# Six attention layers on one core: the transposed probabilities leave PSUM in two copies instead of one

## Chip, core and metric

The kernel runs on one core of one Trainium2 chip. Its metric is the device time of one launch in microseconds (us). Three runs of the kernel before gave 2954.64 us in the median, from 2952.83 to 2957.69.

## What is computed

The network has a first block (16-head attention on 2048 tokens of 128 features, beside an 8-expert layer) and a second block. The second block adds two branches: a selective-scan (Mamba) branch, and six transformer layers. The change lies in the attention of those six layers. Cut to that part, the reference is:

```python
def local_attention(q, k, v):              # WINDOW 32, 16 heads of 64
    bk2, bv2 = (look(bk), look(bv))        # each window of 32 sees itself and the one before
    sim = jnp.einsum('bhwie,bhwje->bhwij', bq, bk2) * QK_SCALE
    sim = jnp.where(mask, -jnp.finfo(sim.dtype).max, sim)
    attn = jax.nn.softmax(sim, -1)
    out = jnp.einsum('bhwij,bhwje->bhwie', attn, bv2)
...
for i in range(DEPTH):                     # DEPTH 6
    x = attn_layer(shift_tokens(x), Wqkv[i], q_scale[i], k_scale[i], Wo[i]) + x
    x = ffn_layer(shift_tokens(x), ln_g[i], ln_b[i], W1[i], b1[i], W2[i], b2[i]) + x
```

Each q and k row is also normalised per head and turned by rotary tables.

## The kernel before

The part that matters here begins some 1190 us into the run. `transformer_pe`, `transformer_dve`, `transformer_act`, `transformer_pool` and `transformer_sp` each write one engine's instruction stream for 96 steps (6 layers of 16 tiles of 128 tokens), and 7 more steps in which only the feed-forward part of the last tiles is left. The order inside a step is written out by hand and is the same in every step. The engines are tied by semaphores alone.

PSUM is used as four pairs of banks (`pair_table`). A pair is 128 partitions by two banks of 512 fp32. On TensorE the helper `pair(key, *until)` names the next user of a pair: it first waits for what the user before had left as `until`, and then stores its own `until` for the one to come.

TensorE (PE) does in step n, in this order:

- `scores_first(n)`: the mask and half of the scores of tile n
- `project_q(n + 2)`, then `scores_second(n)`
- `side(n)`: one transpose, and the output projection of tile n - 1 (line 1438)
- `project_k(n + 2)`
- `turn_probs(n)`: eight 128x128 transposes of the probabilities `k.pr` into a pair (line 1386), four into each bank. The first four wait for the first half of the exponentials and the next four for the second half (`exp`)
- `project("v", n + 1)` (line 1345, 128x512 matmuls)
- `values(n, 0)`: 32 products with 64x32 weight blocks, which the trace lists as 64 matmuls (line 1396). They read chunks 0 to 3 of `k.prT`
- `forward(n)`: a piece of the feed-forward part (lines 1444 to 1459) that cycles over four steps: in steps 0, 1 and 3 of each four two 128x512 products, in step 2 `down` and four transposes. It writes to the pair that held the turned probabilities. In the first six steps there is none
- `values(n, 1)`: the same as `values(n, 0)` on chunks 4 to 7
- `turn_rows` for q and k of tile n + 1 (line 1353), and `turn_out(n)` (line 1405)

VectorE (DVE) does in step n: a scan of the Mamba branch (line 468, from step 22), `shift(n)` (a maximum over the scores, line 1807, and two subtractions, line 1813), `finish(n - 1)` (line 1853), `rotate("q", n + 2)` (lines 1826 to 1828), `turn_probs(n)` (line 1846, the copy of the turned probabilities from PSUM to `k.prT` in SBUF), `rotate("k", n + 2)`, `normalise(n, 0)` and `normalise(n, 1)` (lines 1798 and 1802, which divide the values by the sums of the probabilities), then sums of squares for tile n + 2 (lines 1835 and 1840) and a remainder of the feed-forward part.

ScalarE (ACT) takes the exponential in two halves (`probs`, line 1650), and copies the turned rows of q and k and the turned output.

Of the kernel before, what the change touches and what calls it, by code (L numbers as in the profile page):

```python
# [92 lines left out]
def bcast(ap, at, n):  # L93
    shape = list(ap.shape)
    return ap.unsqueeze(at).broadcast_to(shape[:at] + [n] + shape[at:])
# [1230 lines left out]
def transformer_pe(k):  # L1326
    E, s, ps = k.te, k.sem, k.ps
    held = {}

    def pair(key, *until):  # L1330

        p = k.pair[key]
        for name, value in held.get(p, ()):
            E.wait_ge(s(name), value)
        held[p] = until
        return ps[:, 2 * p:2 * p + 2, :]
# [42 lines left out]
        score_half(n, 1, ps[:, 2 * p:2 * p + 2, :]).then_inc(s("lscore"), 1)  # L1379

    def turn_probs(n):
        to = pair(("turn_probs", n), ("prT", n + 1))
        for c in range(8):
            if c % 4 == 0:
                E.wait_ge(s("exp"), 2 * n + c // 4 + 1)
            mm = E.transpose(to[:, c // 4, c % 4 * P:(c % 4 + 1) * P], k.pr[:, c * P:(c + 1) * P], k.ident[:])  # L1386
        mm.then_inc(s("prob_mm"), 1)

    def values(n, o):
        to = pair((f"values{o}", n), (f"on{o}", n + 1))  # L1390
        E.wait_ge(s("prT"), n + 1)
        E.wait_ge(s(f"vw{n % 2}"), 160 * (n // 2 + 1))
        for c in range(4):
            for w in range(4):
                for i in range(2):
                    mm = E.matmul(to[WIN * w:WIN * (w + 1), i, c * (DH + 1):(c + 1) * (DH + 1)],  # L1396
                                  k.prT[i * DH:(i + 1) * DH, 4 * o + c, WIN * w:WIN * (w + 1)],
                                  k.vw[i * DH:(i + 1) * DH, n % 2, w, 4 * o + c, :], start=True, stop=True, skip_group_check=True)
        mm.then_inc(s(f"values{o}"), 1)
# [145 lines left out]
    for n in range(LAST_STEP):  # L1545
# [10 lines left out]
        if n < NTILE:  # L1556
            turn_probs(n)
        if n + 1 < NTILE:
            project("v", n + 1, ("v_out", n + 2))
        if n < NTILE:  # L1560
            values(n, 0)
# [5 lines left out]
        if n < NTILE:  # L1567
            values(n, 1)
# [216 lines left out]
def transformer_dve(k):  # L1785
    V, s, ps = k.ve, k.sem, k.ps

    def pair(*key):
        p = k.pair[key]
        return ps[:, 2 * p:2 * p + 2, :]  # L1790

    def heads(*key):
        return pair(*key).rearrange("p a (h d) -> p (a h) d", d=DH)
# [11 lines left out]
    def shift(n):  # L1805
        V.wait_ge(s("lscore"), n + 1)
        V.tensor_reduce(k.nmxl[:], heads("scores", n), X_AXIS, ALU.max, negate=True).then_inc(s("v"), k.v.up())
        V.wait_ge(s("v"), k.v.n)
        if n:
            V.wait_ge(s("prob_mm"), n)  # L1810
        for o in range(2):
            of = slice(8 * o, 8 * o + 8)
            V.tensor_tensor(k.pr[:].rearrange("p (h d) -> p h d", d=DH)[:, of, :], heads("scores", n)[:, of, :], bcast(k.nmxl[:, of], 2, DH), ALU.add).then_inc(s("shifted_s"), 1)
# [26 lines left out]
        V.tensor_reduce(k.sx[:, n % 2, :], k.ss[:, n % 2, :, :], X_AXIS, ALU.max).then_inc(s("squares"), 1)  # L1840

    def turn_probs(n):
        V.wait_ge(s("prob_mm"), n + 1)
        if n:
            V.wait_ge(s("values1"), n)
        V.tensor_copy(k.prT[:].rearrange("p c n -> p (c n)"), pair("turn_probs", n).rearrange("p a b -> p (a b)")).then_inc(s("prT"), 1)

    def finish(n):
        l, t = n // NT, n % NT
# [45 lines left out]
    for n in range(LAST_STEP):  # L1895
# [5 lines left out]
        if n < NTILE:  # L1901
            shift(n)
# [8 lines left out]
        if n < NTILE:  # L1911
            turn_probs(n)
# [364 lines left out]
```

## Time and profile before

| | us |
|---|---|
| Median of three runs | 2954.64 |
| The profiled execution, its own time | 2953.88 |
| Its span in the trace | 2951.7 |
| TensorE busy in the span | 2796.9 |
| VectorE busy in the span | 2318.7 |

The span is what the trace shows from its first to its last instruction. The time of an execution is 2.18 us more. TensorE's granted clock averaged 0.992 of full speed (2.4 GHz). Start times in the rows below are us from the start of the span.

### The profile page before, as it was taken

What the parts mean: (1) busy time and instruction counts of PE and PEld (TensorE: products, weight loads), DVE (VectorE), ACT (ScalarE), POOL (GpSimd) and SP (SyncE); (2) the same over time, 40 slices, a digit from 0 to 9 for tenths busy, and PEclk for the clock granted to TensorE, in tenths of its full rate; (3) what the DMA queues carried; (4) which work ended last, traced back from release to release, by engine and by line L of the source; (5) the groups of instructions that cost most, each with busy time, mean ns of one, the idle gap of its engine ahead of it and who ended that gap; (6) DMA issues with size and microseconds to landing.
All of it is one profiled execution on the core that took longest, in us unless ns stands there. A gap on an engine that the chain in (4) does not pass through costs nothing.

```text
span 2951.7 us, 98080 instructions
## 1 busy us (share of the span) xinstructions
PE 2796.9 (95%) x40886; PEld 1837.8 (62%) x40886; DVE 2318.7 (79%) x3704; ACT 1755.5 (59%) x2626; POOL 1677.4 (57%) x1458
## 2 busy tenths in 40 slices
PE   8999999999999998889999999999999999999995
PEld 5556566555665655566666666666666666666664
DVE  6777756684677777989868898889988998888982
ACT  4455555555666665556566666666666666666662
POOL 1000002000566665666667888788887888788872
PEclk9999999999999999999999999999999999999998
DMA  2000000000011121243243434333433343333431
GB/s 95 1 1 1 1 1 3 1 1 10 24 45 47 44 47 45 57 133 76 68 126 85 96 88 117 83 96 90 114 92 82 88 115 93 90 92 85 92 76 47
DMA packets 183064, 188.20 MB, mean 64 GB/s; under 512 B 77470, under 2 KB 130468, under 8 KB 181092
## 3 DMA queue, kind: packets, MB, share of 16 engines
q1 hardware_dynamic: 182628, 181.94, 24.7%
q8 instruction: 328, 5.37, 0.8%
q14 instruction: 108, 0.88, 0.1%
HBM read 61.00 MB, written 6.03 MB: 23 GB/s over the span
## 4 chain that ended last, share of the span: by engine, by line
PE 75%; DVE 11%; issue 5%; SPq 3%; POOL 3%; ACT 2%; DMA 1%; DVEq 0%; POOLq 0%; ACTq 0%
PE ps L1345 14%; PE ps L579 12%; PE ps L1353 5%; PE ps L1396 5%; PE ps L1438 5%; PE ps L1360 4%; PE ps L614 4%; PE ps L592 4%; PE ps L1386 3%; PE ps L1459 2%; PE ps L1405 2%; PE ps L1452 2%; PE ps L526 2%; PE ps L597 2%; DVE nmx L687 2%
## 5 line engine op out<-in xcount | busy, mean ns | idle before, releaser
L1345 PE MATMUL ps<-wqkv,xcT 128*128 128x512 f32 x1152 | 552.7, 602 | 5.8 <-issue 2.4
L579 PE MATMUL ps<-xnT,qp 128*128 128x512 f32 (+3 forms) x1280 | 526.0, 542 | 18.4 <-ACT prob L806 17.6
L1966 POOL TENSOR_TENSOR ra<-ra,rb 128x1024 f32<-128x1024 f32 x191 | 451.3, 2368 | 122.5 <-DVE rb L1828 121.6
L806 ACT ACTIVATE prob<-ps,ebias,shift 128x1024 f32<-128x1024 f32 (+7 forms) x384 | 360.3, 954 | 125.9 <-DVE ebias L696 57.1
L814 ACT ACTIVATE probT<-ps 128x512 f32<-128x512 f32 (+3 forms) x384 | 207.7, 541 | 351.3 <-PE ps L592 351.2
L579 PEld LDWEIGHTS ps<-xnT,qp 128*128 128x128 f32 x1280 | 231.5, 190 | 274.1 <-issue 229.5
L1985 POOL TENSOR_TENSOR ra<-ra,rn 128x1024 f32<-128x1024 f32 x192 | 362.3, 1908 | 8.9 <-DVE ra L1893 1.2
L687 DVE TENSOR_REDUCE nmx<-ps 128x1 f32<-128x1024 f32 (+7 forms) x256 | 245.7, 986 | 109.8 <-PE ps L579 95.1
L1345 PEld LDWEIGHTS ps<-wqkv,xcT 128*128 128x128 f32 x1152 | 196.9, 191 | 155.4 <-issue 144.6
L1607 ACT ACTIVATE sq<-ps 128x1024 f32<-128x1024 f32 x192 | 195.6, 1019 | 89.7 <-PE ps L1345 89.3
L1396 PEld LDWEIGHTS ps<-vw,area 64*32 64x32 f32 x12288 | 138.7, 106 | 163.8 <-issue 162.9
L1826 DVE TENSOR_TENSOR ra<-ps,tab 128x1024 f32<-128x1024 f32 x192 | 233.1, 1214 | 3.6 <-issue 3.1
L1835 DVE TENSOR_REDUCE ss<-sq 128x16 f32<-128x1024 f32 x192 | 224.1, 1208 | 0.0
L592 PE MATMUL ps<-ident,prob 128*128 128x128 f32 x1344 | 218.1, 279 | 5.6 <-ACT probT L814 5.6
L1360 PEld LDWEIGHTS ps<-kT,qT 64*32 64x32 f32 x12288 | 140.7, 105 | 120.3 <-issue 119.4
L592 PEld LDWEIGHTS ps<-ident,prob 128*128 128x128 f32 x1344 | 149.4, 141 | 81.1 <-issue 67.4
L1396 PE MATMUL ps<-vw,area 64*32 64x65 f32 x12288 | 171.2, 225 | 27.9 <-issue 24.2
L1353 PE MATMUL ps<-ident,ra 128*128 128x128 f32 x1536 | 191.5, 278 | 2.4 <-DVE rb L1828 1.2
L705 DVE COPY probT<-ps 128x512 f32<-128x512 f32 (+3 forms) x256 | 150.8, 589 | 54.2 <-PE ps L597 50.5
L1360 PE MATMUL ps<-kT,qT 64*32 64x64 f32 x12288 | 173.6, 224 | 19.6 <-issue 18.7
L1624 ACT ACTIVATE vs<-ps 128x1024 f32<-128x1024 f32 x96 | 98.4, 1025 | 155.6 <-PE ps L1345 149.5
L614 PE MATMUL ps<-probT,vb 128*32 128x128 f32 x4352 | 190.4, 278 | 0.0
(270 smaller groups left out, 5588.8 us busy)
## 6 DMA issues: line engine op xcount, KB each, us to landing
vw<-vs SPq DMA_DIRECT2D x576, 130.0 KB
vw<-vs SPq DMA_DIRECT2D x384, 65.0 KB
bc<-bc_scratch SPq DMA_DIRECT2D x128, 128.0 KB, 3.0
area<-bc_scratch SPq DMA_DIRECT2D x128, 128.0 KB, 4.1
wqkv<-lwqkv_dram SPq DMA_DIRECT2D x6, 1536.0 KB, 9.1
xc<-xs SPq DMA_DIRECT2D x96, 32.0 KB
wo<-lwo_dram SPq DMA_DIRECT2D x6, 512.0 KB, 8.8
area<-ys SPq DMA_DIRECT2D x24, 128.0 KB
```

The lines of the kernel that those rows point to most:

```text
L579: mm = E.matmul(ps[:, 2 * r + o // 512, 0:w], k.qp[:, group % 2, g % NTH * P:(g % NTH + 1) * P], k.xnT[:, k0 + o:k0 + o + w], start=True, ...
L592: mm = E.transpose(ps[:, 4, c * P:(c + 1) * P], k.prob[:, r, c * P:(c + 1) * P], k.ident[:])
L614: mm = E.matmul(ps[32 * c:32 * c + 32, 6 + b, 0:P], k.vb[:, group % 2, block, 0:32] if odd else k.vb[:, group % 2, block, VW:VW + 32], k.p ...
L687: V.tensor_reduce(k.nmx[:, b, mine.index(U):mine.index(U) + 1], of, X_AXIS, ALU.max, negate=True).then_inc(s("v"), k.v.up())
L806: A.activation(k.prob[:, r, 0:nk], ps[:, 2 * r:2 * r + 2, :].rearrange("p a b -> p (a b)")[:, 0:nk], ACT.Exp, bias=k.ebias[:, row % 2:row ...
L1345: mm = E.matmul(to[:, c, :], k.xcT[:, n % 4, :], k.wqkv[l % 2][:, at + 512 * c:at + 512 * (c + 1)], start=True, stop=True)
L1353: mm = E.transpose(to[:, j // 4, j % 4 * P:(j % 4 + 1) * P], k.ra[:, n % 2, w, j * P:(j + 1) * P], k.ident[:])
L1360: mm = E.matmul(to[WIN * w:WIN * (w + 1), o, j * DH:(j + 1) * DH], k.qT[o * DH:(o + 1) * DH, j, WIN * w:WIN * (w + 1)], k.kT[o * DH:(o + 1 ...
L1396: mm = E.matmul(to[WIN * w:WIN * (w + 1), i, c * (DH + 1):(c + 1) * (DH + 1)], k.prT[i * DH:(i + 1) * DH, 4 * o + c, WIN * w:WIN * (w + 1) ...
L1826: V.tensor_tensor(out_a, of, bcast(tab[:, 2 * w, :], 1, H), ALU.mult)
L1966: G.tensor_tensor(k.ra[:, n % 2, w, :], k.ra[:, n % 2, w, :], k.rb[:, w, :], ALU.add).then_inc(s("added_" + what), 1)
L1985: G.tensor_tensor(of, of, bcast(k.rn[:, n % 2, H * w:H * (w + 1)], 2, DH), ALU.mult).then_inc(s("normal_" + what), 1)
```

## The change

The copy of the turned probabilities is split into two copies of 128x512. TensorE raises `prob_mm` after the fourth and after the eighth transpose, where it raised it once after the eighth. VectorE copies the first bank when `prob_mm` says that its four transposes are done and `values0` of the step before has been computed, and then copies the second bank in the same way with `values1`. `prT` now counts two per step. `values(n, 0)` waits for the first copy and `values(n, 1)` for the second. The next user of the PSUM pair waits for both.

```diff
     def turn_probs(n):
-        to = pair(("turn_probs", n), ("prT", n + 1))
+        to = pair(("turn_probs", n), ("prT", 2 * n + 2))
         for c in range(8):
             if c % 4 == 0:
                 E.wait_ge(s("exp"), 2 * n + c // 4 + 1)
             mm = E.transpose(to[:, c // 4, c % 4 * P:(c % 4 + 1) * P], k.pr[:, c * P:(c + 1) * P], k.ident[:])
-        mm.then_inc(s("prob_mm"), 1)
+            if c % 4 == 3:
+                mm.then_inc(s("prob_mm"), 1)

     def values(n, o):
         to = pair((f"values{o}", n), (f"on{o}", n + 1))
-        E.wait_ge(s("prT"), n + 1)
+        E.wait_ge(s("prT"), 2 * n + o + 1)
...
         if n:
-            V.wait_ge(s("prob_mm"), n)
+            V.wait_ge(s("prob_mm"), 2 * n)
...
     def turn_probs(n):
-        V.wait_ge(s("prob_mm"), n + 1)
-        if n:
-            V.wait_ge(s("values1"), n)
-        V.tensor_copy(k.prT[:].rearrange("p c n -> p (c n)"), pair("turn_probs", n).rearrange("p a b -> p (a b)")).then_inc(s("prT"), 1)
+        for o in range(2):
+            V.wait_ge(s("prob_mm"), 2 * n + o + 1)
+            if n:
+                V.wait_ge(s(f"values{o}"), n)
+            V.tensor_copy(k.prT[:, 4 * o:4 * o + 4, :].rearrange("p c n -> p (c n)"), pair("turn_probs", n)[:, o, :]).then_inc(s("prT"), 1)
```

## Rows read from the trace of the kernel before

**Rows 1.** The page: TensorE and VectorE in the span, and the chain's shares by engine.

```profile
PE 2796.9 (95%) x40886; PEld 1837.8 (62%) x40886; DVE 2318.7 (79%) x3704; ACT 1755.5 (59%) x2626; POOL 1677.4 (57%) x1458
...
PE 75%; DVE 11%; issue 5%; SPq 3%; POOL 3%; ACT 2%; DMA 1%; DVEq 0%; POOLq 0%; ACTq 0%
```

**Rows 2.** One stretch of the layers: length, then busy us by engine, clock, DMA.

```profile
1980.00:2260.00 280.00, 271.05 (x5348) 185.29 (x5347) 245.44 (x372) 179.32 (x254) 231.92 (x200) 1.00 0.40 98
```

**Rows 3.** Waits of TensorE, 1170 to 2920 us: in total, times, longest.

```profile
PE ps L1396 <- issue: 24.2, 39, 3.5
PE ps L1360 <- issue: 18.7, 29, 2.0
...
PE ps L1353 <- DVE rb L1828: 1.2, 3, 0.5
```

**Rows 4.** Chain that ended last, around step 47: start, us, what.

```profile
2037.44 0.22 DVE recl L1798
...
2048.50 1.16 PE ps L1386 x8
2049.66 1.72 PE ps L1345 x4
2051.38 0.66 issue
2052.04 1.01 PE ps L1396 x58
```

**Rows 5.** Timeline of step 47: start, us, engine, line, and the wait before.

```profile
2049.49 1.88 PE L1345 MATMUL ps<-wqkv,xcT 128*128 128x512 f32 x4
...
2050.13 0.68 DVE L1828 TENSOR_TENSOR rb<-ps,tab 128x512 f32<-128x512 f32 x1
...
2050.73 1.21 DVE L1846 COPY area<-ps 128x1024 f32<-128x1024 f32 x1
```

**Rows 6.** Timeline of step 46.

```profile
2030.27 1.88 PE L1345 MATMUL ps<-wqkv,xcT 128*128 128x512 f32 x4
...
2031.02 1.21 DVE L1846 COPY area<-ps 128x1024 f32<-128x1024 f32 x1
...
2032.33 0.85 PE L1396 MATMUL ps<-vw,area 64*32 64x65 f32 x64 [0.18 <-issue]
```

**Rows 7.** Timeline of step 49.

```profile
2084.82 1.88 PE L1345 MATMUL ps<-wqkv,xcT 128*128 128x512 f32 x4
...
2085.37 1.21 DVE L1846 COPY area<-ps 128x1024 f32<-128x1024 f32 x1
...
2086.69 0.85 PE L1396 MATMUL ps<-vw,area 64*32 64x65 f32 x64
```

**Rows 8.** Timeline of step 83.

```profile
2690.63 1.88 PE L1345 MATMUL ps<-wqkv,xcT 128*128 128x512 f32 x4
2690.85 1.21 DVE L1846 COPY area<-ps 128x1024 f32<-128x1024 f32 x1
...
2692.45 0.79 PE L1396 MATMUL ps<-vw,area 64*32 64x65 f32 x57
```

**Rows 9.** VectorE by line and shape: count, busy, mean ns, idle before and releaser.

```profile
L1813 DVE TENSOR_TENSOR area<-ps,nmxl 128x512 f32<-128x512 f32 x192 | 123.6, 686 | 3.3
L1807 DVE TENSOR_REDUCE nmxl<-ps 128x16 f32<-128x1024 f32 x96 | 117.2, 1220 | 92.1 <-PE ps L1360 91.6 <-issue 0.4
L1846 DVE COPY area<-ps 128x1024 f32<-128x1024 f32 x96 | 116.4, 1212 | 2.4 <-PE ps L1386 2.4
L705 DVE COPY probT<-ps 128x512 f32<-128x512 f32 x160 | 110.5, 691 | 19.4 <-PE ps L597 17.2 <-issue 0.6
L1798 DVE RECIPROCAL recl<-ps 128x8 f32<-128x8 f32 x192 | 38.5, 201 | 112.4 <-PE ps L1396 112.4
```

**Rows 10.** Timeline, VectorE at one pair of subtractions (merged) and at one division.

```profile
2010.50 1.29 DVE L1813 TENSOR_TENSOR area<-ps,nmxl 128x512 f32<-128x512 f32 x2
...
2019.10 0.21 DVE L1798 RECIPROCAL recl<-ps 128x8 f32<-128x8 f32 x1 [0.50 <-PE ps L1396]
```

**Rows 11.** Timeline of the last step, 95.

```profile
2897.99 1.16 PE L1386 MATMUL ps<-ident,area 128*128 128x128 f32 x8 [0.88 <-ACT area L1650]
2899.19 1.23 DVE L1846 COPY area<-ps 128x1024 f32<-128x1024 f32 x1 [1.22 <-PE ps L1386]
2900.49 0.97 PEld L1396 LDWEIGHTS ps<-vw,area 64*32 64x32 f32 x64 [1.57 <-issue]
2900.52 1.18 PE L1396 MATMUL ps<-vw,area 64*32 64x65 f32 x64 [1.36 <-issue]
```

**Rows 12.** Waits of VectorE, 1170 to 2920 us: in total, times, longest.

```profile
DVE recl L1798 <- PE ps L1396: 112.4, 94, 4.8
DVE nmxl L1807 <- PE ps L1360: 91.6, 59, 6.5
```

## Prediction

> **What bounds the kernel now.** I read the page first, for the busiest engine and the chain that ended last: TensorE is busy for 95% of the span and holds 75% of the chain, VectorE 11% [rows 1]. Then I cut out a stretch of layers: of 280 us TensorE is busy for 271, VectorE for 245, GpSimd for 232 [rows 2]. So TensorE is nearly a solid line, and what a change here can win is a part of its remaining 9 us in 280. The list of its waits says where they lie: the longest item is line 1396, the values, 24.2 us in 39 places, put down to "issue", that is to no releaser which the profile names [rows 3]. The reader should ask what that is. The chain around step 47 has such a place, 0.66 us just ahead of the values [rows 4]. The timeline answers it. In step 47 the projection before ends at 2049.49 + 1.88 = 2051.37, the copy of line 1846 at 2050.73 + 1.21 = 2051.94, and the values start at 2052.04 [rows 4, 5]. In step 46 the copy ends at 2032.23 and the values start at 2032.33 [rows 6]. In both, 0.10 us after the copy: the values wait for the copy, and "issue" hides it. The copy itself is not waiting for the transposes. It starts 0.08 us before the listed end of the rotation of line 1828 (2050.13 + 0.68 = 2050.81), so it follows VectorE's own queue [rows 5].
>
> **How long TensorE waits.** Where the copy is early, as in step 83 (ends 2692.06), the values start at 2692.45, which is 0.06 to 0.07 us before the listed end of the projection, 2692.51 [rows 8]. That is the start without a wait. Measured from there, a step waits 0.17 us plus what the copy ends after the projection. In step 47 the copy is 0.56 us late, and the wait is 0.73. In step 46 it is 0.24. In step 49 the copy ends 0.12 us before the projection (2086.58 against 2086.70), and 0.05 is still lost [rows 7]. Going through the timeline of all 96 steps in this way gives five kinds:
>
> - eleven steps as step 47, each 0.73 us, 8.0 in all
> - six between 0.35 and 0.53, together 2.8
> - thirty between 0.08 and 0.32, as step 46, together 4.5
> - thirty as step 49, about 0.05 each, together 1.5
> - seventeen without a wait, as step 83; and the first and the last step, which stand for themselves
>
> **The change, part by part.** *The first copy.* A 128x512 copy out of PSUM takes 691 ns in the first block of this kernel, where the whole copy here takes 1212 [rows 9]. It starts where the whole copy starts, since VectorE's queue sets that. So the values may start 1.21 - 0.69 = 0.52 us earlier, and a step gains the smaller of its wait and 0.52. From above a gain is bounded by the wait itself (0.73 in the longest kind). From below it would be nothing, if the first copy had to wait for the second half of the transposes or if the release were not the copy.
>
> *The second copy.* Two 128x512 subtractions in a row fill 1.29 us where one takes 686 ns, so they start 0.60 us apart [rows 9, 10]. The two copies then end 1.29 to 1.30 us after the start, 0.08 to 0.09 later than now, and everything behind on VectorE (rotate k, both divisions, the sums of squares) moves by 0.09 in each step. If they did not overlap at all it would be 2 x 0.69 - 1.21 = 0.17. I take 0.09, since every pair of neighbours on VectorE in the rows overlaps, the copy and the rotation before it too [rows 5]. The second half of the values needs the second copy only after the first half (0.85 us) and mostly after a piece of the feed-forward part, so it is not late. The feed-forward piece writes to the pair that the second copy reads. The copy ends 1.30 us after its start, seen on TensorE at 1.40. The first half of the values starts at 0.79 and lasts 0.85, to 1.64, the 0.85 being the length of line 1396 in [rows 6]. That leaves 0.24 us, or some 0.15 for the weight load ahead of the matmul. It costs nothing, but it is thin.
>
> The Trainium skill speaks against such a split. Its page "VectorE: DVE Perf Modes" ("The TRN2 errata", and "Rules for kernel authors") gives a copy from PSUM 120 + N cycles at 0.96 GHz and says to minimise the number of operations. By it the split costs an estimated 120 cycles = 0.125 us a step, 12 us if VectorE were on the path throughout. For one copy it gives 1.19 and 0.66 us, where the rows say 1.21 and 0.69.
>
> *The semaphores.* VectorE gets two more waits a step and TensorE one more increment. Line 1846 already carries two waits and still overlaps the instruction before it [rows 5], so I put these at nothing. The wait for `values0` of the step before has long been met.
>
> *Who pays for the 0.09.* VectorE waits for the values before line 1798 in 94 places, 112.4 us [rows 12]. In an ordinary step it waits 0.50 us before the second division [rows 10]. Moved 0.09 later, with TensorE 0.05 to 0.3 earlier, it still waits. In a step of the 0.73 kind TensorE comes 0.52 earlier and VectorE 0.09 later, 0.61 against 0.50: VectorE starts its second division 0.4 earlier instead of 0.5. What follows it on TensorE is 1.9 us of row transposes before the output is turned, so TensorE keeps its 0.52. In the next step the maximum over the scores waited for TensorE in 59 of 96 steps [rows 12]. The others are mostly the steps after `down`, in which VectorE is late; that chain begins at the second half of the values of the step before (2037.44 in [rows 4]) and so moves forward with it.
>
> *Where it is lost.* In steps 0, 1, 2 and 5 nothing stands between the two halves of the values, and the row transposes then wait for rotate k on VectorE (three waits of line 1353, [rows 3]). There the gain is lost, and 0.09 is added.
>
> *The last step.* It has no projection. The transposes run from 2897.99 to 2899.15, the copy follows at 2899.19, and the values at 2900.52 [rows 11]. VectorE is free, so the first copy can start when four transposes are done, after about half of their 1.16 us, at 2897.99 + 0.58 + 0.04 = 2898.61, and ends at 2899.30. The values start at 2899.40 or a little later: 1.1 us.
>
> **The sum.** Ten steps of the first kind (eleven less step 2) at 0.52 make 5.2. The second kind makes 2.8 less 0.42 for step 5, 2.35. The third kind makes 4.5, the fourth 1.5, the last step 1.1. Together 14.65. Four steps that lose 0.09 take 0.35. That leaves 14.3 us. The profiled execution took 2953.88, so 2939.6; the median is 0.76 above it, so I forecast 2940. That is 0.48% faster.
>
> **The rivals.** *The gain is partly eaten further on.* TensorE has 18.7 us of waits in the scores (line 1360) in 29 places, which I can't explain from any releaser [rows 3]. If something outside the step's order sets those, for example the arrival of its own instructions, an earlier arrival there only waits longer. Also, if the thin 0.15 us of the feed-forward piece is gone, the first kind gives some back. If all that the first two kinds bring is eaten (7.5), 6.8 are left: 2947. Against it: the thirty small waits are spread over steps that have no such stall.
>
> *VectorE becomes what sets the step.* Then nothing is won and each step pays the second copy: 96 x 0.09 = 8.6 us, 2963, slower by 0.3%. It decides if VectorE's idle time in a step is used up. That is (112.4 + 91.6) / 96 = 2.1 us a step [rows 12], against 0.09 more work and about 0.15 a step less of TensorE's time. Only the 37 steps where the maximum waits for nothing speak for it. The page of the Trainium skill named above would make it 12 us, 2966.
>
> *It changes nothing.* The values would be held by something that only ends together with the copy, such as the weight load of line 1396, which lists 1.57 us of idle before it in the last step [rows 11]. Against it: the constant 0.10 us behind the copy, whatever the projection does. Then 2954.
>
> *More comes back than is put in.* An earlier second half of the values brings VectorE's late chain forward, and the 0.21 us which the first kind keeps (0.73 - 0.52) shrinks too if the copy starts earlier against the projection. Eleven times 0.21, and some of the waits for the exponential such as the 0.88 us of the last step [rows 11], would make about 20 us: 2934.
>
> **How the numbers follow.** Differences under 0.2% (5.9 us) can't be told from no change here. The forecast (12 to 17 us gained) has 0.55, partly eaten 0.20, more 0.10, no change 0.10, slower 0.05. Two thirds of "partly eaten" is still over 5.9 us. So faster 0.78, same 0.17, slower 0.05. The range goes from 2935 (19 us, half of the "more" case) to 2950 (4 us, most of "partly eaten").
>
> **What will show it.** Two 128x512 copies a step of about 0.69 us, 0.60 apart, and VectorE's busy time up by 96 x 0.17 = 16 us (the overlap is counted in both). "Issue" before the first half of the values down from 24 us to some 9. In steps such as 47 the values start 0.10 us after the first copy. VectorE's wait before line 1798 falls. The prediction is wrong if the values still start after the second copy, if the feed-forward piece has a new wait, if the waits of line 1360 grow by what the values lose, or if VectorE's waits before lines 1798 and 1807 hardly remain.

## The result, and the profile after

The changed kernel took 2932.60 us in the median of five runs (2927.12 to 2939.50), against 2954.64 for the kernel before in the same comparison (five runs, 2952.83 to 2958.82). The ratio is 0.9930, with a 95% interval from 0.9915 to 0.9944, that is 16.5 to 25 us faster. 2940 was forecast with a range from 2935 to 2950, so the sign is right, and the time lies 2.4 us under the low end of the range.

The page after, TensorE and VectorE in the span of 2930.7 us (before: [rows 1]):

```profile
span 2930.7 us, 98271 instructions
...
PE 2792.3 (95%) x40886; PEld 1835.2 (63%) x40886; DVE 2333.9 (80%) x3800; ACT 1755.6 (60%) x2626; POOL 1685.3 (58%) x1458
```

VectorE has 96 instructions and 15.2 us of busy time more, close to the 16 us that were foretold for the overlap counted twice.

Waits of TensorE from 1170 to 2920 us in the changed kernel, in total, times, longest (before: [rows 3]). The values are line 1397 now and rotate k is line 1829:

```profile
PE ps L1360 <- issue: 14.4, 24, 1.1
PE ps L1386 <- ACT area L1651: 13.7, 14, 2.5
PE ps L1460 <- DVE area L1878: 13.4, 2, 11.3
PE ps L1397 <- issue: 6.2, 13, 1.6
PE ps L1397 <- DMA vw<-vs: 3.1, 3, 1.6
PE ps L1397 <- DVE rb L1829: 2.7, 1, 2.7
PE ps L1353 <- DVE rb L1829: 2.6, 4, 1.1
```

The row of the values with "issue" went from 24.2 us in 39 places to 6.2 in 13. This row holds two things, which its places separate. Before, 15.1 us in 24 places lie ahead of the first half of the values; now 0.3 us in one place, the last step. The other 9.1 us in 15 places were gaps between two matmuls of the second half, where nothing waits for a copy, and 5.9 us in 12 places are left of them. The 3.5 us, the longest place in [rows 3], is one of these. In step 6 of the kernel before:

```profile
1309.46 0.76 PE L1396 MATMUL ps<-vw,area 64*32 64x65 f32 x52
...
1313.70 0.46 PE L1396 MATMUL ps<-vw,area 64*32 64x65 f32 x12 [3.48 <-issue]
```

One place of 2.7 us is now put down to VectorE's rotation; it is the first step, which waited 3.2 us before under the name "issue". Line 1353 waits 1.4 us more, in the first steps, where there is nothing between the two halves of the values. The row of line 1460 is no new wait: its 11.3 us lie behind the last step, and the kernel before has the same wait, of 11.28 us, later than 2920 us. The row with DMA was 1.8 us before. In steps 41 and 73 the values wait 1.07 and 1.57 us for the transfer that fills `vw`, long after the copy.

Timeline of step 47 of the changed kernel (before: [rows 5]):

```profile
2042.10 1.88 PE L1345 MATMUL ps<-wqkv,xcT 128*128 128x512 f32 x4
...
2042.72 0.68 DVE L1829 TENSOR_TENSOR rb<-ps,tab 128x512 f32<-128x512 f32 x1
...
2043.32 1.27 DVE L1848 COPY area<-ps 128x512 f32<-128x512 f32 x2
...
2044.10 1.01 PE L1397 MATMUL ps<-vw,area 64*32 64x65 f32 x64
```

The projection ends at 2043.98. The two copies start at 2043.32 and fill 1.27 us together, so with 0.68 us each they start 0.60 apart. The first ends at 2044.00, and the values start at 2044.10, 0.10 later. What was a wait of 0.73 us is 0.19.

The last step (before: [rows 11]):

```profile
2879.15 1.16 PE L1386 MATMUL ps<-ident,area 128*128 128x128 f32 x8 [0.88 <-ACT area L1651]
2879.82 1.29 DVE L1848 COPY area<-ps 128x512 f32<-128x512 f32 x2 [0.68 <-PE ps L1386]
2880.57 0.72 PEld L1397 LDWEIGHTS ps<-vw,area 64*32 64x32 f32 x64 [0.50 <-issue]
2880.61 0.85 PE L1397 MATMUL ps<-vw,area 64*32 64x65 f32 x64 [0.29 <-issue]
```

The values start 1.46 us after the first transpose, where it was 2.53: 1.07 us, forecast as 1.1.

VectorE by line and shape in the changed kernel (before: [rows 9]):

```profile
L1848 DVE COPY area<-ps 128x512 f32<-128x512 f32 x192 | 122.5, 678 | 1.4 <-PE ps L1386 1.4
L1808 DVE TENSOR_REDUCE nmxl<-ps 128x16 f32<-128x1024 f32 x96 | 117.1, 1220 | 77.1 <-PE ps L1360 76.6
L1799 DVE RECIPROCAL recl<-ps 128x8 f32<-128x8 f32 x192 | 38.5, 201 | 88.7 <-PE ps L1397 88.4
```

VectorE's idle time before the divisions fell from 112.4 to 88.7 us and before the maximum from 92.1 to 77.1. It has not become what sets the step.

To see where the time went, I took the stretch from the first matmul of the values in step 0 to that of step 95 in each profile, and summed over all steps what TensorE lost at four places: ahead of the first half of the values (from step 1 on, measured from the start without a wait, as in the prediction), ahead of the transposes, and in gaps between matmuls within the second half of the values and within the scores (starts more than 0.09 us apart, less the usual 0.01). Three profiles of each kernel, two of them from the runs below, in us:

```
kernel            stretch  ahead of values  ahead of turns  within values 2  within scores
before             1700.7             20.1            14.7             13.6           25.4
before (b_again)   1695.9             21.4            14.1             12.0           22.0
before (b_third)   1693.9             20.5            16.0             11.4           18.6
after              1678.6              6.1            16.0              9.3           20.2
after (a_again)    1682.3              5.4            16.4              9.8           22.5
after (a_third)    1682.1              5.9            17.3             10.3           22.0
```

The means are 1696.8 and 1681.0, 15.8 us apart. The waits ahead of the values give 14.9 of it, where the prediction's terms came to 14.65. The stalls within the second half of the values give 2.5, those within the scores 0.4, and the waits ahead of the transposes take 1.6 back. Of the 5.4 to 6.1 us that are left ahead of the values, 2.2 to 2.8 are steps 41 and 73, in which the copy is not what is awaited.

TensorE's clock is not the cause. In this stretch it was granted 1.2 GHz in place of 2.4 for 13.6, 17.0 and 13.6 us in the three profiles before and for 10.2, 13.6 and 13.6 us in the three after. The means are 2.3 us apart. At half the clock that is at most 1.1 us of time, by an estimate from the two levels.

### The profile page after: what moved, and what is told of

Its sections match the earlier page's. It is cut to its first block, busy times and chain, and to the rows that moved or that the text cites. A ratio compares the mean times of both kernels' runs of the same rounds, so it can differ in the third digit from the quotient of the medians.

```text
span 2930.7 us, 98271 instructions
## 1 busy us (share of the span) xinstructions
PE 2792.3 (95%) x40886; PEld 1835.2 (63%) x40886; DVE 2333.9 (80%) x3800; ACT 1755.6 (60%) x2626; POOL 1685.3 (58%) x1458
## 4 chain that ended last, share of the span: by engine, by line
PE 73%; DVE 10%; issue 5%; SPq 4%; POOL 4%; ACT 3%; DMA 1%; DVEq 0%; POOLq 0%; ACTq 0%
PE ps L1345 13%; PE ps L579 13%; PE ps L1353 5%; PE ps L1397 5%; PE ps L1439 4%; PE ps L1360 4%; PE ps L614 4%; PE ps L592 4%; PE ps L1386 2%; PE ps L1406 2%; PE ps L526 2%; PE ps L1460 2%; PE ps L1453 2%; PE ps L597 2%; DVE nmx L687 2%
## 5 line engine op out<-in xcount | busy, mean ns | idle before, releaser
L1439 PE MATMUL ps<-wo,area 128*128 128x128 f32 x1536 | 188.0, 275 | 1.7 <-ACT area L1657 1.2
L1651 ACT ACTIVATE area<-area 128x512 f32<-128x512 f32 x192 | 117.6, 630 | 119.1 <-DVE area L1814 119.1
```

Source lines behind the costliest of these rows:

```text
L1439: mm = E.matmul(to[:, 0, 0:P], k.oT[:, c * P:(c + 1) * P], k.wo[:, l % 2, c, :], start=c == 0, stop=c == 7, skip_group_check=True)
```

## The experiments

All times are medians; ratios are to the kernel before, run in the same comparison. The kernel before gave 2954.64, 2949.89, 2947.34 and 2951.10 us in the four comparisons. The last three ran on three different chips, and the changed kernel was a part of the first two alone. So where a later kernel is set beside the changed one, its runs come from another comparison.

**The two kernels again.** Nothing is edited.

> The changed kernel once more, nothing edited. In its first profile the waits of TensorE ahead of the first half of the values fell by 14.6 us (16.7 to 2.1), as forecast, and 7 to 9 us more came from stalls inside the dense runs of values and scores (39 us before, 30 after). Theory P: the 14 us belong to the change and are there again; the stalls inside the runs vary from execution to execution and are not the change's, so in this profile they lie anywhere from 28 to 42 us, overlapping with the kernel before, and the time is 2930 to 2942. Rival Q: the change shortens these stalls too; then they are again near 30 here and near 39 in a repeat of the kernel before, and the time is 2932 again.

> The kernel before once more, nothing edited, as a null and for a second profile. Both theories: ratio 1.000 within 0.2%, 16 to 17 us of waits ahead of the first half of the values. Theory P: stalls inside values and scores anywhere in 28 to 42 us. Rival Q: near 39 us again.

The changed kernel took 2933.09 us, ratio 0.9935 (0.9922 to 0.9949). The kernel before took 2947.16, ratio 0.9993 (0.9982 to 1.0003). The waits ahead of the values, 5.4 and 21.4 us, are within 1.3 us of those of the first pair. The expectation's 16 to 17 us counts without the last step and without steps 41 and 73; counted so, the 21.4 are 17. The stalls within both kinds of dense runs were 39 us in the first profile of the kernel before and 34 in this one; after the change they were 30 and 32. Theory P is nearer: the 39 did not come again, so a part of the 9 us between the first two profiles was chance, and a smaller part remains to be explained.

**Two copies, late release.**

```diff
-        E.wait_ge(s("prT"), 2 * n + o + 1)
+        E.wait_ge(s("prT"), 2 * n + 2)
```

> Two copies as in the changed kernel, but both halves of the values wait for both copies. Theory P: the whole gain is the earlier release of the first half of the values. Here the release comes 0.08 to 0.09 us later than in the kernel before in some 77 steps, so the waits ahead of the first half grow from 16.7 to about 23 us and the time is 2954.6 + 6 = 2961 (ratio 1.002). Rival R: the split itself brings something (other PSUM timing, shorter stalls inside the runs); then it is at or below the kernel before, ratio 0.997 to 1.000.

It took 2954.64 us, ratio 1.0009 (0.9999 to 1.0019), against 2949.89 for the kernel before. The first half of the values waits for the second copy, as the timeline of step 47 shows:

```profile
2050.41 1.88 PE L1345 MATMUL ps<-wqkv,xcT 128*128 128x512 f32 x4
...
2051.64 1.28 DVE L1848 COPY area<-ps 128x512 f32<-128x512 f32 x2
...
2053.01 0.85 PE L1397 MATMUL ps<-vw,area 64*32 64x65 f32 x64 [0.73 <-issue]
```

The copies end at 2052.92, the values start at 2053.01. The waits ahead of the values sum to 23.9 us, 3.2 more than the mean of the kernel before, and the stretch is 1700.1 us. So the split alone brings nothing; the gain is the earlier release. Theory P had 6 us of cost for the split. The ratio says 3, with an interval that reaches from nothing to 6.

**TensorE's instructions 128 places further on.** Changed kernel, with

```diff
     E.wait_ge(s("band"), 1)
+    for i in range(128):
+        E.wait_ge(s("band"), 1)
     turn_rows("q", 0)
```

> The changed kernel with 128 more satisfied waits in TensorE's instruction stream ahead of the first tile of the layers, so that every later instruction sits 128 places further on. In the profiles of both kernels the stalls inside values and scores of over 0.1 us stand at the same place modulo 256 in TensorE's stream, 2.2 to 3.0 us after the start of an instruction transfer. Theory F: they are waits for the next block of instructions, so they move to other steps here, stand at the same place modulo 256 again, and their sum changes (anything from 15 to 50 us, the time with it); the added waits themselves cost under 3 us. Rival: they belong to certain steps of the work (memory or PSUM contention); then the same steps stall as in the changed kernel and the time is the same but for the added waits.

It took 2939.64 us, ratio 0.9957 (0.9943 to 0.9970). The added waits cost 7 us, not under 3, a miss: the trace has them as 64 records, most with two waits each, that start 0.106 us apart from 1185.43 to 1192.46. The first values start at 1211.4 us, 9.4 later than in the changed kernel. The rest fits the clock, which fell behind the waits: 1190 to 1200 us was granted 0.59 of full speed in the mean, where the changed kernel has 1.00. The row has the busy times by engine and then the clock:

```profile
1190.00:1200.00 10.00, 6.57 (x90) 5.11 (x91) 6.10 (x9) 2.87 (x6) 3.72 (x6) 0.59 0.04 8
```

 The stretch from the first values on is 1677.2 us, 3.8 under the changed kernel's mean. The trace lists 84,269 weight loads, matmuls and semaphore instructions of TensorE, against 84,205 in the changed kernel: only 64 more for the 128 waits. By this count nearly all stalls stand at place 193 or 194 of 256 in all profiles, here too. So each such place should now come 64 records earlier in the work, that is by 32 pairs of weight load and matmul. It does. In step 34 the second half of the values stops after 13 matmuls, where it stopped after 45 (the rows of the changed kernel are in the last section):

```profile
1823.32 0.33 PE L1397 MATMUL ps<-vw,area 64*32 64x65 f32 x13
...
1825.22 0.75 PE L1397 MATMUL ps<-vw,area 64*32 64x65 f32 x51 [1.57 <-issue]
```

In step 37 the stop is after 27 matmuls instead of 59, in step 50 after 29 instead of 61, and within the scores of step 36 after 20 instead of 52. Where 32 fewer lie outside the same run (scores of steps 10 and 20), the stall is gone. It is gone too in the scores of steps 5 and 8, where the place now comes after 9 and 27 matmuls, and others are new (steps 1, 14, 21 and 30). So a passage decides where a stall can be, and not that there is one. Theory F holds: these are passages to the next block of instructions, and each resume comes 2.2 to 3.0 us after the start of a transfer on the queue of instructions. The sum within values and scores is 32 us, as in the changed kernel: the shift changed the places but not the total. It changed the shares, though: 14.6 us within the second half of the values and 17.3 within the scores.

**One more VectorE instruction a step.** Changed kernel, with

```diff
+        V.memset(k.spare[:, n % 2, :], 0.0)
```

behind the second copy.

> The changed kernel with one more VectorE instruction in each step, a memset of 128x512 to a spare tile behind the second copy (some 0.3 to 0.6 us). It leaves the first copy where it is. Theory P: VectorE has slack behind the copies (it waits 0.4 to 0.5 us ahead of the second division and before the maximum in 54 steps), so of 96 x 0.3 to 0.6 = 29 to 58 us of added work only 2 to 10 us come through: 2935 to 2943. Rival V: VectorE sets the step since the change, and nearly all of it comes through: over 2955.

The memset took 485 ns in the mean, 46.6 us in all. The time was 2939.55 us, ratio 0.9977 (0.9966 to 0.9987), and the stretch 1690.3 us, 9.3 more than the changed kernel's mean. TensorE waits 3.1 us more ahead of the values and 2.4 us more ahead of the transposes. By the stretch a fifth of the added work comes through, but this profile is of the slowest of twelve runs, 8 us over their median. By the medians of the two kernels it is 6.5 us, a seventh; by their ratios, of different comparisons, 13. So the share lies between a seventh and somewhat over a quarter. Theory P holds, rival V is excluded, and VectorE is not free.

**Four copies instead of two.** Changed kernel, with

```diff
-            V.tensor_copy(k.prT[:, 4 * o:4 * o + 4, :]...
+            for h in range(2):
+                ins = V.tensor_copy(k.prT[:, 4 * o + 2 * h:4 * o + 2 * h + 2, :]...
+            ins.then_inc(s("prT"), 1)
```

> The changed kernel with four copies of 128x256 instead of two of 128x512; the first half of the values still waits for the first half, now the second of four copies. Theory P: a further split costs VectorE 0.07 to 0.09 us each, so the release comes 0.08 us later and the second half 0.16; the waits ahead of the first half of the values rise from 5.5 to 7 or 8 us and the time by 1 to 4 us (2934 to 2938). Rival (an operation's fixed cost weighs on the whole step): 192 more operations at 0.125 us come through, 24 us: 2957.

It took 2934.83 us, ratio 0.9954 (0.9941 to 0.9967). The copies of 128x256 took 411 ns and start 0.33 us apart, so a further split costs VectorE 0.07 us. The waits ahead of the values were 6.4 us, where 7 or 8 were expected. A rise of 1 to 4 us is inside the noise of this comparison; 24 us is excluded.

**The late chain of VectorE.** In every fourth step the second half of the values goes ahead of the feed-forward piece, once in the changed kernel and once in the kernel before:

```diff
+        if n % 4 == 2 and 6 <= n < NTILE:
+            values(n, 1)
         forward(n)
...
-        if n < NTILE:
+        if n < NTILE and not (n % 4 == 2 and n >= 6):
             values(n, 1)
```

> The changed kernel, but in every fourth step (n % 4 == 2, from step 6) TensorE computes the second half of the values ahead of the feed-forward piece. There VectorE waited 1.9 us for these values, and was then late for the scores of the next step; TensorE waits 15 us in all for the exponentials, mostly in these next steps. Theory P (late VectorE chain): these waits fall by 4 to 8 us, so 2926 to 2931. Rival F (instruction blocks): two dense runs of 128 instructions each now follow each other without long matmuls between, and the stalls inside the values grow by 5 to 15 us, so that nothing is won or it is slower: 2932 to 2942.

> The same reorder of every fourth step in the kernel before, with its one copy. Theory P: the reorder's gain comes on top of what it has, and part of the copy's lateness (the eleven steps that waited 0.73 us) goes with it, so it gains a little more than in the changed kernel: 5 to 12 us, 2938 to 2945. Rival F: as above, 2948 to 2958.

They took 2942.01 us, ratio 0.9982 (0.9972 to 0.9992), and 2964.81 us, ratio 1.0057 (1.0045 to 1.0070). Both are slower than without the reorder, the second outside what either theory gave. The timeline of step 46 of the first of the two shows why:

```profile
2036.62 0.86 PE L1397 MATMUL ps<-vw,area 64*32 64x65 f32 x64
2036.73 1.02 ACT L1627 ACTIVATE vs<-ps 128x1024 f32<-128x1024 f32 x1 [1.57 <-PE ps L1345]
...
2037.81 0.75 PE L1397 MATMUL ps<-vw,area 64*32 64x65 f32 x50 [0.32 <-ACT vs L1627]
...
2039.49 0.34 PE L1397 MATMUL ps<-vw,area 64*32 64x65 f32 x14 [0.94 <-issue]
```

The second half writes to the PSUM pair of the projection, which ScalarE is still copying out: a wait of 0.32 us. Then, after 50 matmuls, comes a stall of 0.94 us. Summed over the reordered steps 10 to 90, the wait is 8.2 us and the stalls within the second half went from 1.7 to 7.1. The waits ahead of the transposes of the next steps fell as theory P said, from 5.1 or 5.5 to 2.2 us. Rival F was right about the stalls, and the wait for ScalarE was in neither theory. In the kernel before with the reorder the stalls within the second half are 25.2 us in all, against 12.3 without it. Its stretch is 1715.7 us, 19 more than without the reorder, and a part of that is the clock: TensorE was granted 1.2 GHz for 34.0 us of it, where the three profiles without the reorder have 13.6 to 17.0. By an estimate from the two levels that is up to 10 us, which neither theory had.

**Released at three quarters.** The kernel with four copies, but `values(n, 0)` waits for the third:

```diff
-        E.wait_ge(s("prT"), 2 * n + o + 1)
+        E.wait_ge(s("prT"), 4 * n + o + 3)
```

> Four copies of 128x256, and the first half of the values waits for the third of them, though it needs only two. In an ordinary step the release then comes about 0.36 us before the listed end of the projection, still early enough for the array (0.17 is the bound), but 0.3 us later than in the changed kernel. Theory S: TensorE's instruction stream stands still at an unmet wait, so a later release delays the next transfer of instructions even where the array does not wait; the stalls inside the second half of the values (8 to 10 us in four profiles with an early release, 12 to 15 in three with a late one) rise to 11 to 15, and with 3 to 5 us more of waits in the steps with a late copy the time is 2939 to 2944. Rival N: these stalls only vary at random or follow the array's own waits; then they stay at 8 to 10 us and the time is 2936 to 2939.

It took 2944.79 us, ratio 0.9980 (0.9969 to 0.9992), just over the 2944 of theory S. The waits ahead of the values were 12.6 us, 6 to 7 more than in the changed kernel, more than the 3 to 5 expected: the third copy ends 0.22 us before the projection in the median step, and in one step of ten over 0.4 us after it. The stalls within the second half of the values were 10.8 us, at the edge of what theory S gave. To settle this I took one more profile each of four kernels:

> A third profile of the kernel before, for the stalls inside the second half of the values alone (13.6 and 12.0 us in the first two). Theory S (they grow with the time of release): 11.5 to 14. Rival N (random): anywhere from 8 to 15.

> A second profile of the kernel with two copies and the late release (15.3 us of these stalls in the first). Theory S: 12.5 to 16. Rival N: 8 to 15, as likely below 12 as above.

> A second profile of the kernel that releases at the third of four copies (10.8 us). Theory S: 10 to 12.5, between the early and the late releases again. Rival N: 8 to 15.

> A third profile of the changed kernel (9.3 and 9.8 us). Theory S: 8 to 10.5. Rival N: 8 to 15.

They gave 11.4, 10.9, 13.5 and 10.3 us, in 2951.59, 2956.16, 2945.43 and 2939.09 us. Three of the four missed the narrow windows of theory S (the kernel before by 0.1, the late release lower, the three quarters higher), and all are within rival N's, so a growth in steps is not shown. Two groups can be told apart, though they were drawn after the numbers were seen: the seven profiles with the release around the end of the projection (one copy, or the second or third copy awaited) have 10.8 to 15.3 us, mean 12.5, and the five with the release half a microsecond ahead (the changed kernel three times, the one with four copies, and the one with the memset) have 7.9 to 10.3, mean 9.2. They do not overlap, nor do they without step 6, whose stall of 1.7 to 3.7 us is the largest in each: 8.5 to 12.2 us against 6.3 to 7.7. The kernel with the added waits has 14.6 us there in spite of its early release; its blocks fall into other runs, so it belongs to neither group. With that reserve, 2.5 to 3 us of these stalls go with a late release. The sum of both kinds of stalls doesn't separate (39, 34 and 30 us before, 30, 32 and 32 after). That an earlier release brings the next block of instructions earlier, as theory S has it, is argued and not shown.

**The copy on ScalarE.** ScalarE copies the first half, or both halves, right behind its squares of k; or the kernel before has its single copy moved there. For the first:

```diff
+    def probs_turned(n, o):                                  # ScalarE
+        A.wait_ge(s("prob_mm"), 2 * n + o + 1)
+        if n:
+            A.wait_ge(s(f"values{o}"), n)
+        A.activation(k.prT[:, 4 * o:4 * o + 4, :].rearrange("p c n -> p (c n)"), pair("turn_probs", n)[:, o, :], ACT.Copy).then_inc(s(f"prT{o}"), 1)
...
-        for o in range(2):                                   # VectorE
+        for o in (1,):
```

> ScalarE copies the first half (behind its squares of k), VectorE only the second. VectorE has 0.60 us less to do in each step, and the first copy no longer stands behind its rotations. Theory P (late VectorE chain): what the memset of 0.49 us cost, 6.6 us, comes back in the same measure, about 4 to 7 us, and most of the 5.5 us of waits ahead of the first half go: 2923 to 2929. Rival A: ScalarE then comes late with the copies of the values and of the turned rows, and it is 2933 or more.

> ScalarE copies both halves, VectorE none: VectorE has 1.2 us less in each step, ScalarE 1.1 us more. Theory P: 8 to 13 us below the changed kernel, 2920 to 2926, with TensorE's waits for the exponentials down from 16 to 10 us. Rival A: ScalarE comes late for the copy of the next values and delays the second half of the values or the row copies: 2933 or more.

> The kernel before with its one copy moved from VectorE to ScalarE, not split. In an ordinary step it ends about 0.5 us before the projection, so the array does not wait. Theory P: moving does the same as splitting and more, so it is within 3 us of the kernel with both halves on ScalarE, 2921 to 2929; by theory S it keeps 2 to 4 us more of stalls in the second half of the values than that one. Rival A: as there, 2933 or more.

They took 2916.80 us, ratio 0.9893 (0.9873 to 0.9914); 2917.18 us, ratio 0.9884 (0.9865 to 0.9903); and 2921.13 us, ratio 0.9902 (0.9887 to 0.9917). All three beat both kernels: the slowest of their twelve runs took 2924.52 us, the fastest of the changed kernel 2926.94. The first is 6 us under the range that was expected of it, the second 3 us under its own, and the third at the low end. Timeline of one ordinary step of the kernel with both halves on ScalarE:

```profile
2009.44 1.88 PE L1345 MATMUL ps<-wqkv,xcT 128*128 128x512 f32 x4
2009.69 1.08 ACT L1657 ACTIVATE area<-ps 128x512 f32<-128x512 f32 x2
...
2011.25 0.70 PEld L1397 LDWEIGHTS ps<-vw,area 64*32 64x32 f32 x64 [0.76 <-issue]
2011.25 0.86 PE L1397 MATMUL ps<-vw,area 64*32 64x65 f32 x64
2011.36 1.03 ACT L1625 ACTIVATE vs<-ps 128x1024 f32<-128x1024 f32 x1 [0.59 <-PE ps L1345]
```

Both copies are done at 2010.77, 0.55 us before the projection's end, and ScalarE still waits 0.59 us for its next work. Its waits of VectorE show the room that was made:

```profile
DVE recl L1808 <- PE ps L1397: 191.4, 100, 4.9
DVE nmxl L1817 <- PE ps L1360: 87.3, 57, 6.6
```

The stretch is 1664.6, 1661.3 and 1673.1 us for the three, 16, 20 and 8 us under the changed kernel. The waits ahead of the values are 3.2, 3.2 and 6.0 us, the stalls within the second half of the values 7.9, 7.2 and 5.8, within the scores 14.9, 14.5 and 20.2. The unsplit copy on ScalarE does not have more stalls in the values than the split one, which theory S had asked for; it has them in the scores. Of the 16 and 20 us, then, 9 and 10 are fewer stalls of the two kinds (22.8 and 21.7 us against 31.4 in the mean of the changed kernel), and 2.6 are waits ahead of the values. Of the rest, 5 and 7 us, a part is the clock: TensorE was granted 1.2 GHz for 6.8 and 0 us of the stretch, against 12.5 in the mean of the changed kernel, by estimate up to 3 and 6 us.

Theory P's own mechanism isn't seen: the waits ahead of the transposes, which are those for the exponentials, did not fall from 16 to 10 us. In the list they are 12.4 us with both halves on ScalarE, and 13.7 in the changed kernel. Nor can the fewer stalls within the scores be put down to the copy. The first two kernels have one more wait in each step, and the trace lists 84,275 instructions of TensorE, 70 more than in the changed kernel, so their blocks fall into other places. The third has the changed kernel's 84,205, and with 20.2 us about its stalls within the scores.

## Why the prediction was right or wrong

- **What the 24 us of "issue" were.** Right for 15.1 us of them. There the values waited for the copy, 0.10 us behind it, and with the release put back (both_wait) the waits were back. The other 9.1 us were stalls within the second half of the values. The prediction took the whole row for the wait ahead of them.
- **The sum.** Right for the terms that it has. They came to 14.65 us, and the waits ahead of the values fell by 14.9, the last step by 1.07 of the 1.1. The first copy took 678 ns where 691 was taken from another stage, and the copies start 0.60 apart as taken from the subtractions. The five kinds leave out step 41 with 1.21 us, which is a wait for a transfer, so nothing was lost by it.
- **The sign "down from 24 us to some 9".** Met by luck. The rows give 6.2 + 2.7, but 5.9 of that are the stalls within the second half.
- **The losses in the first steps.** Right in kind. Line 1353 waits 1.4 us more.
- **VectorE has room.** Right in kind, and underpriced. The memset put a price on it: of 46.6 us of added work some 6.5 to 13 come through. By that share, an estimate, the 8.6 us that the second copies add cost 1.2 to 2.4, and the waits ahead of the transposes grew by 1.6. The prediction had 0.35.
- **The feed-forward piece behind the second copy.** No new wait. Its one "issue" place of 0.9 us in the list of the changed kernel stands behind the last step, and the kernel before has it too, after 2920 us.
- **The rival "more comes back than is put in".** Its 2934 is nearest to the 2932.60, and that is luck. VectorE's late chain was to shorten the waits for the exponentials; ahead of the transposes they rose from 14.9 to 16.6 us.
- **The range failed, by two steps.** The first is a term put at nothing: TensorE's stalls at the passages between blocks of instructions. The prediction saw them in the scores, as 18.7 us without a releaser, and named them in its first rival only as something that eats the gain; those within the second half of the values it took for waits for the copy. The runs showed the opposite sign. In the first pair of profiles the stalls fell by 9.5 us, most of it chance, and in three pairs by 2.9 us in the mean (2.5 within the second half of the values, 0.4 within the scores). 14.9 + 2.9 less 1.6 is 16.2, beside the 15.8 us between the stretches.
- The second step is the base. The sum was made against one execution of 2953.88 us and carried to a median of three, 2954.64. Over 64 runs in four comparisons and 11 as b_again, the kernel before took 2939 to 2959 us, with a median of 2949.5, and the changed one 2927 to 2940 in eleven runs, with a median of 2933.1. The range was built from mechanisms alone and left out that the kernel's own executions scatter by more than 10 us (21 runs of one comparison: 2945.30 to 2958.04). By these medians the gain is 16.4 us where 14.3 was forecast, and the base was 5 us high. That is most of the 7.4 us between 2940 and 2932.60. Whether the base was high by chance or by the chip of the first comparison is open. The measured ratios, 0.9930 and 0.9935, stand for 19 to 21 us; the 3 to 5 us between these and the profiles are not assigned. The interval of the second reaches down to 15 us, that of the first only to 16.5.

## What to carry to other kernels

When a wait is listed without a releaser, set the end of the suspected producer beside the start of the waiter over several instances: a constant distance names it. Do so for every place of the row, and look whether it stands ahead of the group or within it: one row can hold two causes. Then ask why the producer is late. Here it stood behind other work in the queue of a busy engine, and moving it to an engine that was idle at that moment brought one and a half to two times what splitting it did, a part of which is the clock and the places of the blocks. Before a range is given, look at the scatter of the kernel's own runs, and do not take a median of three as the base.

## What the runs showed of the hardware

- TensorE stalls at fixed places of its instruction stream, one in every 256 recorded instructions: 48 to 61 stalls of over 0.09 us within values and scores, 30 to 39 us in all, in the seven profiles of the two kernels and of the shifted one. Of those over 0.2 us, 47 of 49 in the kernel before and all 41 in the changed one end 2.2 to 3.0 us after the start of a transfer on the instruction queue. Not each passage stalls. In the second halves of scores and values of the changed kernel it matters how far into the 64 matmuls the passage falls: of 32 passages within the first 16 matmuls one stalls, of 70 further on 43. A shift of the stream by 64 recorded instructions moved the passages by 32 matmuls. An example in the kernel before is the second half of the values of step 34:

```profile
1820.25 0.69 PE L1396 MATMUL ps<-vw,area 64*32 64x65 f32 x45
...
1822.35 0.42 PE L1396 MATMUL ps<-vw,area 64*32 64x65 f32 x19 [1.41 <-issue]
```

and the same place in the changed kernel:

```profile
1815.45 0.69 PE L1397 MATMUL ps<-vw,area 64*32 64x65 f32 x45
...
1816.96 0.42 PE L1397 MATMUL ps<-vw,area 64*32 64x65 f32 x19 [0.81 <-issue]
```

  Both stop after 45 matmuls, though the steps start 5 us apart. The Trainium skill ("Runtime: NRT & Kernel Launch", "Instruction fetch mechanics") says that instructions come in blocks of 256 and that crossing a block is mostly hidden. The block agrees with the 256 places here. That it is hidden does not hold in runs of 128 instructions that take 0.85 us.
- Satisfied waits on TensorE are not free: 128 written in a row took 7 us. The trace lists 64 instructions for them, 0.106 us apart, so that is 0.05 us for each wait as written. Behind these 7 us without a matmul the granted clock fell to 1.2 GHz, and 1190 to 1200 us had 0.59 of full speed in the mean.
- Two copies from PSUM of 128x512 by VectorE start 0.60 us apart and end 1.27 us after the start of the first, against 1.21 for one of 128x1024; of 128x256 they start 0.33 us apart. On ScalarE two of 128x512 fill 1.08 us.
